# Local attention in a chain of sixteen blocks: the projections of the next sequence start two units earlier, and stacked queries and keys signal apart

## The reference

```
h = shift_token(x)                       # second half of the features from the token before
q, k, v = split(h @ wqkv)                # 8 heads of 64
q, k = l2norm(q) * qs, l2norm(k) * ksc
q, k = rotary_xpos(q, k)                 # q*cos*scale + rotate_half(q)*sin*scale
sim  = bq @ look_around(bk)^T            # windows of 64: this window and the one before
out  = softmax(mask(sim)) @ look_around(bv)
x    = x + out @ wo
```

## Time and profile before

| | us |
|---|---|
| three runs | 8457.02, 8472.45, 8474.06 |
| median | 8472.45 |
| span of the profiled execution | 8469.3 |
| PE busy | 6094.0 (72%) |
| DVE busy | 4274.2 (50%) |
| ACT busy | 3054.3 (36%) |
| POOL busy | 1907.5 (23%) |

### The profile page before, as it was taken

How to read it: one execution, slowest core, us unless ns; L and a number is a source line. 1 busy time by engine, 2 the same in 40 slices (tenths; PEclk the granted TensorE clock), 3 DMA queues, 4 the chain that set the end, 5 groups by cost and what they waited for, 6 DMA issues and landing times. The chain is left out here.

```text
span 8469.3 us, 123982 instructions
## 1 busy us (share of the span) xinstructions
PE 6094.0 (72%) x46161; PEld 3016.1 (36%) x46352; DVE 4274.2 (50%) x6846; ACT 3054.3 (36%) x6729; POOL 1907.5 (23%) x1689
## 2 busy tenths in 40 slices
PE   5557567876678876665789997777776666677677
PEld 3445251115432222222345443443443333344343
DVE  4324436653357647888544444444445555444444
ACT  1002323553335614433112223553543333354453
POOL 0112042113232104444110001432420000242341
PEclk6558677887778987877868878998997777899898
DMA  1001013211111000000032221111100000110110
GB/s 42 4 32 46 22 55 77 66 53 52 57 54 39 26 14 0 0 0 0 7 60 51 51 50 29 37 30 41 37 23 7 0 0 0 36 38 24 45 39 23
DMA packets 261149, 269.25 MB, mean 32 GB/s; under 512 B 113472, under 2 KB 190657, under 8 KB 258689
## 3 DMA queue, kind: packets, MB, share of 16 engines
q1 hardware_dynamic: 250368, 240.70, 11.0%
q0 software_dynamic: 10240, 21.25, 0.8%
HBM read 123.03 MB, written 71.66 MB: 23 GB/s over the span
## 5 line engine op out<-in xcount | busy, mean ns | idle before, releaser
L2170 PE MATMUL ps<-s_l2b_hc,ident 128*128 128x512 f32 x512 | 362.2, 847 | 331.9 <-DVE s_l2b_hc L2333 331.9
L1942 DVE TENSOR_REDUCE s_l3l_negmax<-ps 128x4 f32<-128x512 f32 x256 | 175.0, 684 | 743.3 <-PE ps L1783 743.3
L2118 POOL TENSOR_TENSOR s_l2b_Bx<-s_l2b_du,s_l2b_B 128x512 f32<-128x512 f32 x256 | 406.6, 1610 | 473.9 <-ACT s_l2b_B L2240 411.0
L1783 PE MATMUL ps<-s_l3l_qk 64*64 64x64 f32 (+1 forms) x5632 | 298.0, 256 | 287.1 <-DMA s_l3l_qk<-s_l3l_rope 267.9
L1873 ACT ACTIVATE s_l3l_probs<-ps,s_l3l_biases,s_l3l_q_inverse 128x128 f32<-128x128 f32 x1024 | 455.6, 462 | 53.0 <-DVE s_l3l_biases L1944 52.6
L2325 DVE TENSOR_TENSOR_SCAN s_l2b_state<-s_l2b_decay,s_l2b_Bx 128x512 f32<-128x512 f32 x256 | 390.0, 1563 | 155.2 <-ACT s_l2b_decay L2246 113.3
L1721 POOL TENSOR_TENSOR s_l3l_probs<-s_l3l_probs,s_l3l_inverse 128x512 f32<-128x512 f32 x256 | 267.1, 1043 | 828.6 <-DVE s_l3l_inverse L1923 828.4
L1745 PE MATMUL ps<-s_l3l_hs,s_l3l_wqk 128*128 128x512 f32 x512 | 304.3, 702 | 177.8 <-DVE s_l3l_prod L1897 95.4
L1057 DVE TENSOR_REDUCE s_L3a_negmax<-ps 128x1 f32<-128x128 f32 (+3 forms) x512 | 236.2, 488 | 345.6 <-PE ps L893 343.1
L638 DVE TENSOR_REDUCE s_L1a_negmax<-ps 128x1 f32<-128x512 f32 x512 | 316.6, 682 | 149.0 <-PE ps L501 148.2
L1035 ACT ACTIVATE s_L3a_pt<-ps 128x256 f32<-128x256 f32 (+3 forms) x512 | 195.3, 434 | 513.3 <-PE ps L893 511.5
(11 more groups left out here) (654 smaller groups left out, 14161.8 us busy)
## 6 DMA issues: line engine op xcount, KB each, us to landing
s_l3l_qk<-s_l3l_rope SPq DMA_DIRECT2D x1024, 64.0 KB
scratch_rope<-s_L3a_rope SPq DMA_DIRECT2D x32, 512.0 KB, 2.8
ks<-scratch_parts SPq DMA_DIRECT2D x384, 32.0 KB
s_L3a_qs<-scratch_rope SPq DMA_DIRECT2D x64, 128.0 KB
ks<-scratch_rope SPq DMA_DIRECT2D x64, 128.0 KB
s_L0e_slots<-scratch_sent SPq DMA_DIRECT2D x16, 396.0 KB, 5.6
s_L1e_slots<-scratch_sent SPq DMA_DIRECT2D x16, 396.0 KB, 5.7
scratch_square<-s_L1a_rows SPq DMA_DIRECT2D x24, 256.0 KB, 3.0
```

What stands on the lines that cost most here:

```text
L1783: mm = pe.matmul(out[rows, P * k + at:P * k + at + size], t["qk"][rows, b % 2, c, 64 * m:64 * m + 64], t["qk"][rows, b % 2, 4 + c, key:key ...
L2118: pool.tensor_tensor(t["Bx"][:, n % 2, k, :], t["du"][:, b % 2, k, :], t["B"][:, n % 2, :], ALU.mult).then_inc(s["bx_ready"], 1)
L2170: pe.matmul(ps[:, 4 + k, :], g["ident"][:, :], t["hc"][:, n % 2, k, :], start=(n == 0), stop=(n == STATES - 1)).then_inc(s["summed"], 1)
```

## The change

The preparation is moved two units forward: `beside(b, u)` takes the table's entry u + 2 and, for units 6 and 7, entries 0 and 1 of the sequence but one ahead. The projections 0 and 1 of the second sequence come before the units of the first. `shift` moves from unit 4 to unit 3; v 1 and v 3 change places. The semaphore `stacked` is split: POOL waits for the stacked queries alone before it overwrites the query part of `rope`, and for the keys alone before the key part; PE and SP wait for both.

| unit | beside it before | beside it now |
|---|---|---|
| 0 | proj 0 of the next sequence | proj 2 of the next |
| 1 | proj 1 | proj 3 |
| 2 | proj 2 | norm, v 3 |
| 3 | out of the last sequence, proj 3 | out of the last, v 0, v 1 |
| 4 | norm, v 1 | pick 0, pick 1 |
| 5 | v 0, v 3 | qinv, v 2 |
| 6 | pick 0, pick 1 | proj 0 of the next but one |
| 7 | qinv, v 2 | proj 1 of the next but one |

```
-             "scores_ready ... stacked v_shifted
+             "scores_ready ... q_stacked k_stacked v_shifted
+    EARLY = 2
     def prep(b, u):
-        if b == BATCH:
+        if not 0 <= b < BATCH:
             return []
...
+    def beside(b, u):
+        u += EARLY
+        return prep(b + 1 + u // UNITS, u % UNITS)
+    FIRST = [item for u in range(UNITS) for item in prep(0, u)] + [item for u in range(EARLY) for item in prep(1, u)]
...
-        STACKED = 16 * 32
+        STACKED = 16 * 16
...                                      # SP
-                sp.wait_ge(s["stacked"], START + b * STACKED)
+                sp.wait_ge(s["q_stacked"], START + b * STACKED)
+                sp.wait_ge(s["k_stacked"], START + b * STACKED)
-  .then_inc(s["stacked"], 16)
+  .then_inc(s["q_stacked" if e < 2 else "k_stacked"], 16)
...                                      # POOL, rotate(b, e)
-                pool.wait_ge(s["stacked"], START + b * STACKED)
+                pool.wait_ge(s["q_stacked" if e < 2 else "k_stacked"], START + b * STACKED)
...                                      # POOL, before the units, then beside them
+            for e in range(EARLY):
+                rotate(1, e)
-                    if u < 4 and b + 1 < BATCH:
-                        rotate(b + 1, u)
-                    if u == 4 and b + 2 < BATCH:
+                    for ahead, e in ((b + 1, u + EARLY), (b + 2, u + EARLY - UNITS)):
+                        if 0 <= e < 4 and ahead < BATCH:
+                            rotate(ahead, e)
+                    if u == 3 and b + 2 < BATCH:
                         shift(b + 2)
...                                      # PE, ACT, DVE alike
-                    for item in prep(b + 1, u):
+                    for item in beside(b, u):
```

More of the change, by code:

```diff
@@ L1596, in local_attention @@
                "probs": ([P, LAG + 1, 4, P], F32), "turned": ([P, 2, T], F32), "o": ([P, PAIRS, T], F32)}
-    names = ("loaded pool pool_ready tables_ready shifted ready6 ready7 taken6 taken7 squared rope_made rows_floored rows_ready stacked v_shifted "
+    names = ("loaded pool pool_ready tables_ready shifted ready6 ready7 taken6 taken7 squared rope_made rows_floored rows_ready q_stacked k_stacked v_shifted "
              "scores_ready found max_ready exp_ready inverse_ready probs_ready turned_ready turned_taken pv_done o_taken")
+    EARLY = 2
     def prep(b, u):
-        if b == BATCH:
+        if not 0 <= b < BATCH:
             return []
@@ L1606, in prep @@
         if u == 4:
-            return [("norm", b), ("v", b, 1)]
+            return [("norm", b), ("v", b, 3)]
         if u == 5:
-            return [("v", b, 0), ("v", b, 3)]
+            return [("v", b, 0), ("v", b, 1)]
         if u == 6:
@@ L1612, in prep @@
         return [("qinv", b), ("v", b, 2)]
+    def beside(b, u):
+        u += EARLY
+        return prep(b + 1 + u // UNITS, u % UNITS)
+    FIRST = [item for u in range(UNITS) for item in prep(0, u)] + [item for u in range(EARLY) for item in prep(1, u)]
     def order():
-        for u in range(UNITS):
-            yield from prep(0, u)
+        yield from FIRST
         for b in range(BATCH):
@@ L1621, in order @@
                     yield ("out", b - 1)
-                yield from prep(b + 1, u)
+                yield from beside(b, u)
         yield ("out", BATCH - 1)
@@ L1673, in _ @@
                             at = 64 * r + 32 * ab
-                            sp.dma_start(t["qk"][at:at + 32, b % 2, 4 * (e // 2) + c, :], t["rope"][32 * k:32 * k + 32, e, ab, :]).then_inc(s["stacked"], 16)
+                            sp.dma_start(t["qk"][at:at + 32, b % 2, 4 * (e // 2) + c, :], t["rope"][32 * k:32 * k + 32, e, ab, :]).then_inc(s["q_stacked" if e < 2 else "k_stacked"], 16)
         @block.gpsimd
@@ L1772, in scores @@
                 if u == 0:
-                    pe.wait_ge(s["stacked"], START + (b + 1) * STACKED)
+                    pe.wait_ge(s["q_stacked"], START + (b + 1) * STACKED)
+                    pe.wait_ge(s["k_stacked"], START + (b + 1) * STACKED)
                 pe.wait_ge(s["exp_ready"], START + max(4 * (U - 1), 0))
@@ L1811, in values @@
                 mm.then_inc(s["pv_done"], 1)
-            for u in range(UNITS):
-                for item in prep(0, u):
-                    side(item)
+            for item in FIRST:
+                side(item)
             for U in range(BATCH * UNITS + BEHIND):
@@ L1857, in take @@
                     taken_by(act.activation(t["v"][:, b % 2, kt, :], out, ACT.Copy), item)
-            for u in range(UNITS):
-                for item in prep(0, u):
-                    take(item)
+            for item in FIRST:
+                take(item)
             for U in range(BATCH * UNITS + LAG):
@@ L1946, in _ @@
                     invert(U - 1)
-                    for item in prep((U - 1) // UNITS + 1, (U - 1) % UNITS):
+                    for item in beside((U - 1) // UNITS, (U - 1) % UNITS):
                         if item[0] in ("proj", "norm"):
                             take(item)
-                for item in prep(b + 1, u):
+                for item in beside(b, u):
                     if item[0] in ("pick", "qinv"):
```

## The result

The changed kernel takes 8254.77 us in the median of four runs (8243.43 to 8270.78), the kernel before 8472.85 us on the same chip: ratio 0.9747, 95% interval 0.9732 to 0.9761, or 218 us less. The forecast was 258 us less, 8214 us; 8254.77 lies inside the range of 8178 to 8285. The profiled execution took 8243.43 us, with a span of 8241.7 us against 8469.3 before.

What follows compares the result with a forecast made beforehand. Bound: at sequence boundaries PE waits for a chain of pick, 16 SP issues and the last landing. Gains of 44.6 + 10.5 + 9.4 = 64.5 us a call, 258 in four, take 8472.45 to 8214 us; range 8178 to 8285.

Steps and rivals of the forecast that it cites:

- The wait: Sequence boundary: keys there at 15.3 us, PE arrives at about 16.9, so the wait goes with 1.6 us to spare.
- rival 2: Keys still late at 24 boundaries: the spare 1.6 us does not hold, one us each, about 8245; chance 0.09.
- rival 4: Boundary waits as before: unit 6's rotation stands at POOL's head until the stacking is done; 8472, chance 0.02.
- the signs: What would show it right: among others, PE's stacking-DMA wait falls from 279.8 to about 50 us, middle sequences 45 to 48.
- The moved units: Every instruction kept, moved beside another unit; a middle sequence then takes 46.7 us against 55.6 before.
- rival 5: Slower: with projection units in a row the granted clock no longer comes up to 1.0; 8665 us, chance 0.03.
- Units 0 and 1 (proj 2, proj 3): 5.8 and 5.9: Lengths in us of units 0 and 1, set by the loop PE, DVE product, bank free, PE.
- Rival 3: The lock: DVE's floor of the norms meets POOL's rotation, 1.14 us more in 28 sequences; 8246, chance 0.04.
- POOL's lateness: Unit 0's scaling, queued behind the shifted values, is 2.7 us late; via `prod` 0.7 us reaches unit 2, making it 7.3.
- Rival 1: POOL's late scaling of unit 0 delays PE's transposes, the 2.7 us come through in full; 8310, chance 0.10.
- The balance: Sum for a call: gains of 44.6 (middle), 10.5 (first) and 9.4 (seventh sequence), 64.5 us; four calls give 258.

Runs made afterwards that it cites:

- value copies spread: Changed kernel with POOL's two copies of the shifted values put behind the scalings of units 5 and 6, one each: 8199.05 us, ratio 0.969.
- the memset: Changed kernel with POOL's two copies that make the shifted values replaced by memsets of the same tiles: 8216.03 us, ratio 0.9707.
- bias with one input: Changed kernel with DVE's bias product replaced by a reduction reading only the inverse norms, one input from SBUF: 8227.63 us, ratio 0.9714.

## Why the prediction was right, and what its sum missed

**The wait.** Right. The forecast had PE arrive at the next scores with 1.6 us to spare. In the trace after, SP's last issue to the keys starts 13.7 us behind the opening of unit 4 at 5337.23. Before the change PE went on 2.0 us after the start of that issue; by that the keys are there at about 5352.9, and PE loads for the next scores at 5354.28, 1.4 us later:

```profile
L1683 SPq DMA_DIRECT2D s_l3l_qk<-s_l3l_rope x16: 507/591/1347, 5340.7 to 5350.9; - x16
```

Over the 24 middle boundaries this spare is 1.2 us in the median and 0 to 1.8 in range; at the two with none left the load stands for 0.46 and 0.34 us instead of 0.24. So rival 2 came close, but it is out, and so is rival 4. One unit less of distance and 4.06 us of waiting are back. The residue of some 4 us in the seventh sequences is there too: its unit 7 lasts 5.9 to 7.3 us instead of a bare 2.5. What the signs had wrong is the first sequences: 8.7 us of waiting were to stay in each, "about 50" in all, but the two projections put ahead of the units leave 0.2 to 1.0, and 22 in all.

**The moved units.** Right: out in unit 3 takes 8.75 (8.8), unit 5 3.56 (3.8), unit 6 4.38 (4.5). In unit 3 the addition starts 4.82 us into the unit, as reckoned, and the reciprocal ends ahead of it:

```profile
5329.81 3.35 DVE L1913 RECIPROCAL s_l3l_rows<-s_l3l_rows 128x512 f32<-128x512 f32 x1
...
5333.30 0.69 DVE L1928 TENSOR_TENSOR h<-h,ps 128x512 f32<-128x512 f32 x1
```

Unit 4 is 0.34 over its 4.78; the rest is small. Projection units in a row hold a clock of 1.00 when no copy delays one of them (units 6, 7, 0 and 1 with the value copies spread), so rival 5 is out.

**The failed step: "Units 0 and 1 (proj 2, proj 3): 5.8 and 5.9".** Unit 1 took 7.87 in the mean. Its price came from the earlier trace rows, where no value copy lies beside the unit. The working did put the copies there, from 6.2 to 9.6 us behind unit 0's opening, but followed only POOL's own queue: the late scaling and its cover. It did not ask which DVE instruction, due at 6.6, would start inside POOL's 1.88 us. Rival 3 had the port but at the wrong instruction, the floor. The 28 floors beside the units last 395 to 398 ns, before and after, so none was held. (The prediction read the 1533 ns of the earlier trace rows as one case of 32, but a maximum doesn't tell how many there are: the trace before has two floors of 1.5 us and two of 0.5 to 0.6, all four in the preparation before the units.)

The Trainium skill ("SBUF — State Buffer", section "Who interferes with whom") has the rule that was needed, one line from the one that was cited: a DVE instruction with two SBUF inputs contends with a GpSimd instruction that reads SBUF, and not with one that only writes it, and tensor_reduce doesn't contend on trn2. The trace agrees on all three: 0.17 becomes 1.48 us beside the copy, 0.16 beside the memset, 0.16 for the reduction beside the copy.

**POOL's lateness.** Right as a mechanism, but not seen in the changed kernel. Unit 2 is 6.57, without the 0.7, because unit 1 had already grown by more than that; with the lock out of the way (bias with one input) the 0.71 stands in the trace, behind a scaling that starts 3.79 us into unit 1 instead of the 1.13 it is due at, 2.66 us late for the 2.7 reckoned. Rival 1, the lateness through the scaling and the transposes, appears nowhere; its 8310 is out.

**The balance.** The forecast of a call was 42.1 + 5 x 46.7 + 45.4 = 321.0 us, the four stretches average 327.9: 6.9 us too little, 27.7 in four calls. Middle sequences make 20 x 1.3 = 26 of it, the seventh ones 4 x 1.6 = 6.4, and the first ones give back 4 x 1.2 = 4.8: their unit 0 lasts 3.3 us for the 5.4 reckoned (5.8 - 1.3 + 0.9), their unit 1 2.1 us more than its 5.9. The 24 units 1 behind a boundary last together 47 us more than the 5.91 of a unit 0; 24 x 1.12 = 27 of that is the delay, the other 20 the clock; the missing 0.7 of unit 2 covers 24 x 0.7 = 17. With memsets for the copies, the middle and the seventh sequence come out at 46.7 and 45.4, the forecast's own figures, and the time at 8216 against 8214; part of that is chance, since the 0.8 of its unit 2 comes from the bias product beside a rotation (7.14) and from three cold units (8.8), not from `prod`.

The remaining 11 us between the changed kernel's profiled run (8243) and its median (8255) were not followed up: which units 1 go cold changes from run to run, but unprofiled runs don't show it.

## What to carry to other kernels

When an instruction is moved, list not only what queues behind it on its own engine but what every other engine starts during its length; for POOL copies look for DVE instructions with two inputs in SBUF, however small. A line's longest instruction beside its median gives such a place away: here 769 ns beside 166, in the trace of the kernel before. A tiny instruction that heads a chain (here 0.17 us, 128x4) can stretch a unit by more than its own length many times over, and a copy with slack is best put where its neighbour has only one such input, as the spread copies were. The distance of a prefetch is worth what it leaves over the longest latency behind it: here one unit gave 1.1% (with a heavier unit 3), two gave 2.5%, and putting the copies elsewhere 3.1 to 3.4%.

## What was not expected of the hardware

A 128x4 product was held for 1.3 us by a copy that was moving other data, and the delay shows as the product's own duration, not as a wait: no releaser is named, only a mean of 321 ns instead of 175 and a longest of 1478 beside a median of 166 give it away.

PE's idle time of 2.36 us inside a unit, against the usual 1.12, was enough for a fall from 2.4 to 1.2 GHz in 12 of 20 units and not in the other 8 of the same kernel; eight unused products of 1.90 us in all, in that idle time, prevented every fall in a unit 1 and saved some 25 us (medians of 8226.58 against 8251.3 on one chip) although PE had more to do.
